# Second attention of a four-layer kernel: the global keys as a block diagonal, the exponentials of the globals as stationary operand

## What is computed

```python
Q = (x @ Wq.T + bq).reshape(Bb, Ll, H, Dh)      # H = 16 heads of Dh = 8, Ll = 256 tokens, 16 batches
K = (x @ Wk.T + bk).reshape(Bb, Ll, H, Dh)
V = (x @ Wv.T + bv).reshape(Bb, Ll, H, Dh)
...
s_loc = jnp.einsum('blhd,blwhd->bhlw', Q, Kw) * scale       # Kw: the 65 keys around each query
a_loc = jax.nn.softmax(s_loc, axis=-1)
local = jnp.einsum('bhlw,blwhd->blhd', a_loc, Vw)
Kg = K[:, global_indices]                                   # 25 global keys
Vg = V[:, global_indices]
s_g = jnp.einsum('blhd,bghd->bhlg', Q, Kg) * scale
a_g = jax.nn.softmax(s_g, axis=-1)
glob = jnp.einsum('bhlg,bghd->blhd', a_g, Vg)
out = 0.7 * local + 0.3 * glob
return out.reshape(Bb, Ll, Dm) @ Wo.T + bo
```

## Time and profile before

| | us |
|---|---|
| median of 3 runs | 1109.99 (1107.80 to 1113.35) |
| the profiled execution | 1111.69 |
| its span in the trace | 1109.9 |
| PE busy | 961.9 (87%) |
| DVE busy | 784.3 (71%) |
| POOL busy | 681.8 (61%) |
| ACT busy | 578.1 (52%) |

### The profile page before, as it was taken

One profiled execution on the slowest core, in us unless ns is written; L12 is line 12 of the kernel. 1 busy time (PEld: TensorE's weight loads), 2 busy tenths in 40 slices (PEclk: granted clock), 3 DMA queues, 4 the chain that ended last, 5 costly groups with the idle time before them and its releaser, 6 DMA issues.

```text
span 1109.9 us, 27990 instructions
## 1 busy us (share of the span) xinstructions
PE 961.9 (87%) x7664; PEld 709.4 (64%) x7664; DVE 784.3 (71%) x3615; ACT 578.1 (52%) x1250; POOL 681.8 (61%) x1491
## 2 busy tenths in 40 slices
PE   2999999999959995899999999999999419999950
PEld 1777777777734552677777777777776317877730
DVE  3788888888826786457776878777776327888845
ACT  2466676666621432255555555555555107777734
POOL 3566666666631222266768787888878623777765
PEclk9899999999978998599999999999999659999985
DMA  6121211111032442121112121222111157777717
GB/s 182 27 52 27 49 40 35 45 30 45 23 133 88 170 152 86 29 49 28 47 29 59 38 59 37 60 55 59 52 40 36 43 177 226 240 252 245 234 56 212
DMA packets 71376, 98.36 MB, mean 89 GB/s; under 512 B 13688, under 2 KB 43256, under 8 KB 71104
## 3 DMA queue, kind: packets, MB, share of 16 engines
q1 hardware_dynamic: 61040, 83.31, 25.6%
q0 software_dynamic: 4992, 10.30, 2.7%
q10 hardware_dynamic: 5232, 3.42, 1.2%
HBM read 49.48 MB, written 24.77 MB: 67 GB/s over the span
## 4 chain that ended last, share of the span: by engine, by line
PE 74%; DVE 9%; issue 6%; SPq 3%; DMA 3%; POOL 2%; ACT 2%; DVEq 0%; ACTq 0%; POOLq 0%
PE bank L348 6%; PE bank L172 5%; PE bank L253 4%; PE bank L357 4%; PE bank L378 4%; PE bank L1499 4%; PE bank L1500 4%; PE bank L1501 4%; PE bank L1265 4%; PE bank L412 4%; PE bank L419 3%; PE bank L168 3%; PE bank L352 3%; PE bank L387 3%; PE bank L404 2%
## 5 line engine op out<-in xcount | busy, mean ns | idle before, releaser
L536 ACT ACTIVATE p<-bank 128x480 f32<-128x480 f32 (+1 forms) x448 | 240.4, 540 | 256.3 <-PE bank L378 101.0
L671 DVE CUSTOM_DVE_ANT_0 bank<-bank,band 128x160 f32<-128x160 f32 x512 | 157.1, 348 | 80.7 <-PE bank L348 67.9
L671 DVE CUSTOM_DVE_ANT_0 bank<-bank,causal 128x128 f32<-128x128 f32 (+1 forms) x512 | 169.8, 388 | 56.4 <-PE bank L352 40.6
L901 POOL TENSOR_SCALAR_AFFINE_SELECT p<-p 128x380 f32<-128x380 f32 (+1 forms) x256 | 146.6, 602 | 63.2 <-ACT p L536 62.3
L1677 POOL DMA_INDIRECT y_rows<-p,rows x92 | 108.3, 1177 | 64.0 <-DVE p L1630 42.7
L671 DVE DVE_READ_ACCUMULATOR2_ANT nm<- 128x1 f32 x1024 | 145.5, 142 | 0.1
L882 POOL TENSOR_SCALAR_AFFINE_SELECT p<-p 128x256 f32<-128x256 f32 (+1 forms) x192 | 91.1, 486 | 69.1 <-ACT p L536 64.2
L348 PE MATMUL bank<-ks,qs 128*128 128x186 f32 x512 | 116.2, 311 | 3.1 <-issue 1.6
L348 PEld LDWEIGHTS bank<-ks,qs 128*128 128x128 f32 x512 | 79.6, 196 | 35.9 <-issue 21.0
L378 PE MATMUL bank<-qs,ks 128*128 128x160 f32 x512 | 100.4, 299 | 0.0
L1570 ACT ACTIVATE p<-bank,wb 128x512 f32<-128x512 f32 x92 | 63.6, 691 | 39.4 <-PE bank L1501 24.3
(11 more groups left out here) (209 smaller groups left out, 2369.0 us busy)
## 6 DMA issues: line engine op xcount, KB each, us to landing
qs<-parts SPq DMA_DIRECT2D x46, 512.0 KB
qs<-qf SPq DMA_DIRECT2D x128, 128.0 KB, 2.4
rows<-xr SPq DMA_DIRECT2D x23, 260.0 KB
parts<-ks SPq DMA_DIRECT2D x8, 512.0 KB
xs<-x_b SPq DMA_DIRECT2D x16, 256.0 KB
p<-in_w SPq DMA_DIRECT2D x12, 256.0 KB
xin<-in_x SPq DMA_DIRECT2D x16, 128.0 KB, 2.2
parts<-qf SPq DMA_DIRECT2D x4, 512.0 KB
```

Source lines behind the costliest of these rows:

```text
L536: act.activation(pb[:, :, :].rearrange("p u c -> p (u c)")[:, lo:lo + cols], bank[:, 0:cols], ACT.Exp, scale=SCALE).then_inc(L.exp_done, 1)
L671: return dve.tensor_tensor_reduce(at, at, mask, -1.0, -BIG, ALU.add, ALU.min, nm[:, item:item + 1])
L901: pool.affine_select(out=at, in_=at, compare_op=ALU.is_ge, fill=0.0, base=base, pattern=[[0, 4], [sign, hi - lo]], channel_multiplier=-sig ...
```

## The change

All of it lies in the second attention.

- The global keys are written by DVE as a block diagonal, `T.kg[p]`, 128 x (4 x 32) for each t, in one masked operation (`lay_out_kg`, behind unit (1,2)), one iteration after `keep_kg`. `keep_kg` now has two operations instead of three, and each signals `kg_kept`: pass one (0,0) waits for the first, (0,2) for the second.
- The scores of the globals are four fp32r matmuls of 256 columns in each batch, two in unit (2,3) and two in unit (3,3), each with 128 outputs. They read the queries as they were before their spreading, `T.qf`, which becomes a ring of three; so the rows of the maxima are sent to `qf` too, by a second DMA in each quarter. Units (0,3) and (1,3) of pass two are gone.
- Their exponentials are two of 512 columns instead of four of 256. The product with the values, `global_values`, has the exponentials stationary and the masked values (64 columns) moving: eight fp32 matmuls at (0,0) of the next iteration, behind `round_pj`. Its result has tokens on the partitions, so the copy `ogs` and `round_og` are gone, and DVE reads PSUM bank 7 in `normalise`.
- `keep_vg` is one operation instead of four, and `keep_array_busy` issues two matmuls instead of four.
- The diagonal keys and two parts of the `qf` ring share memory with buffers of the last layer.

```diff
+    def unit2(self, i, j, u):
+
+        if not self.local:
+            return 3 * (4 * i + j - 3) + u
+        if i == 0:
+            return u
+        return 3 + 14 * (i - 1) + (0, 3, 6, 10)[j] + (u if j < 3 or i < B else u - 3)
...
+    def pass2_unit(self, local, j, u):
+
+        if local and u == 3:
+            return self.late and j > 1
+        return self.pass2[j] and u < 3
...
-        def round_og():
-            bank_read("og", i, p, th)
-            pe.wait_ge(L.ov_kept, L.kept * fin + 2)
+        def global_values():
+
+            pe.wait_ge(L.exp_done, L.unit2(i - 1, 3, 3) + 1)
+            pe.wait_ge(L.vg_kept, fin + 1)
+            wait(pe, L.on_done, fin)
             for tau in range(2):
-                for r in range(2):
-                    m = turn(T.mi[0][:, (2 * tau + r) * P:(2 * tau + r + 1) * P],
-                             T.ogs[:, r, tau * P:(tau + 1) * P])
-            m.then_inc(L.ot_done, 1)
+                out = T.og[:, tau * S:(tau + 1) * S].rearrange("p (r t z) -> p r t z", r=2, t=4)
+                for t in range(4):
+                    m = pe.matmul(out[:, :, t, :], T.pg[t // 2][:, t % 2 * S + tau * P:t % 2 * S + (tau + 1) * P],
+                                  T.vgb[p][:, t, :].rearrange("p (r z) -> p r z", r=2),
+                                  start=tau == 0 and t == 0, stop=True, skip_group_check=True)
+            m.then_inc(L.pg_done, 1)
...
-            for _ in range(4):
+            for _ in range(2):
                 pe.matmul(T.s1[0][:, 0:P], T.ident[:], T.ident[:], start=True, stop=True)
...
-                    pe.wait_ge(L.kg_kept, i + 1)
+                    pe.wait_ge(L.kg_kept, 2 * i + 1)
+            if L.local and u == 2 and j == 0:
+                pe.wait_ge(L.kg_kept, 2 * i + 2)
...
+            unit = L.unit2(i, j, u)
+            bank = T.s2[unit % 2 if L.local else (j + u) % 2]
...
+                pe.wait_ge(L.mrow[js], L.q_base + L.rows_sent * (batch + 1))
...
             if L.local and u == 3:
-                for t in range(4):
-                    m = pe.matmul(bank[32 * t:32 * t + 32, 0:S], T.kg[par][:, t, :], q[:, t, :].bitcast(F32),
-                                  start=True, stop=True)
+                pe.wait_ge(L.kd_done, i)
+                for c in range(2):
+                    t = 2 * (j - 2) + c
+                    m = pe.matmul(bank[:, c * S:(c + 1) * S], T.kg[n][:, t, :], T.qf[(i - 1) % 3][:, t, :],
+                                  start=c == 0, stop=True, skip_group_check=True)
...
-            if part == 2:
-                if j == 0:
-                    pe.wait_ge(L.vg_kept, i)
-                pe.wait_ge(L.exp_done, 4 * step + 4)
-                m = pe.matmul(T.og[:, r * S:(r + 1) * S], T.vgb[n][:, j, :], pb[:, 3, 0:S],
-                              start=j == 0, stop=False, skip_group_check=True)
...
-                if j == 0 and u == 2 and th.finish and L.local:
-                    round_og()
+                if j == 0 and u == 0 and th.finish and L.local:
+                    global_values()
...
+                if th.pass2_unit(L.local, j, u):
                     pass2(j, u)
-                if th.late and u > 0:
+                if th.late and u in (1, 2):
...
-            if L.local:
-                act.copy(T.ogs[:, :, :], T.og[:, :].rearrange("p (r q) -> p r q", r=2)).then_inc(L.ov_kept, 1)
...
-                act.copy(T.qf[:, :, tau * P:(tau + 1) * P], from_).then_inc(L.q_kept, 1)
+                qf = T.qf[(i + 1) % 3 if L.local else 0]
+                act.copy(qf[:, :, tau * P:(tau + 1) * P], from_).then_inc(L.q_kept, 1)
...
+            if L.local and u == 3:
+                wait(act, L.pg_done, i - 1)
+                act.activation(T.pg[j - 2], bank[:, :], ACT.Exp, scale=SCALE).then_inc(L.exp_done, 1)
+                return
...
-            glob = T.mi[0][:, :].rearrange("p (h c) -> p h c", c=16)
+            glob = T.og[:, :].rearrange("p (h c) -> p h c", c=16)
...
-            dve.wait_ge(L.ot_done, L.kept * fin + 2)
+            dve.wait_ge(L.pg_done, fin + 1)
...
-            wait(dve, L.pv_done, 4 * (i - 1))
-            vg = T.mi[1][:, 0:D].rearrange("p (t r s d) -> p r s t d", t=4, r=2, s=2)
-            out = T.vgb[p][:, :, :].rearrange("p (r s) (t z c) -> p r s t z c", r=2, t=4, z=2)
-            mask = T.diag[:, :].rearrange("p (t d) -> p t d", t=4)
-            for s in range(2):
-                for r in range(2):
-                    m = dve.tensor_tensor(out[:, r, s, :, s, 0:DH], vg[:, r, s, :, :], mask, ALU.mult)
-            m.then_inc(L.vg_kept, 1)
+            wait(dve, L.pg_done, i - 1)
+            vg = T.mi[1][:, 0:D].rearrange("p (t j d) -> p t j d", t=4, j=4)
+            out = T.vgb[p][:, :, :].rearrange("p t (j c) -> p t j c", j=4)
+            mask = T.diag[:, :].rearrange("p (o j d) -> p o j d", o=1, j=4).to_broadcast([P, 4, 4, DH])
+            dve.tensor_tensor(out[:, :, :, 0:DH], vg, mask, ALU.mult).then_inc(L.vg_kept, 1)
 
         def keep_kg():
 
 
             dve.wait_ge(L.kg_done, i + 2)
             kg = T.mi[1][:, 0:4 * 32].rearrange("p (t g) -> p t g", t=4)
-            for lo in (0, NGE + S):
-                dve.tensor_copy(T.ks[n][:, :, lo:lo + NGE], kg[:, :, 0:NGE])
-            dve.tensor_scalar(T.kg[n][:, :, 0:NG], kg[:, :, 0:NG], T.rows[:, 0:1], None,
-                              ALU.add).then_inc(L.kg_kept, 1)
+            dve.tensor_scalar(T.ks[n][:, :, 0:NGE], kg[:, :, 0:NGE], T.rows[:, 0:1], None, ALU.add).then_inc(L.kg_kept, 1)
+            dve.tensor_copy(T.ks[n][:, :, NGE + S:KW], kg[:, :, 0:NGE]).then_inc(L.kg_kept, 1)
...
+        def lay_out_kg():
+
+
+            wait(dve, L.p2_done, L.unit2(i - 1, 3, 3) + 1 if i > 1 else 0)
+            own = [P, 4, 4, NG]
+            keys = T.ks[p][:, :, 0:NG].bitcast(F32).rearrange("p t (o g) -> p t o g", o=1).to_broadcast(own)
+            mask = T.diag[:, ::DH].rearrange("p (a j o) -> p a j o", a=1, o=1).to_broadcast(own)
+            dve.tensor_tensor(T.kg[p].rearrange("p t (j g) -> p t j g", j=4)[:, :, :, 0:NG], keys, mask,
+                              ALU.mult).then_inc(L.kd_done, 1)
...
                     normalise()
                 if j == 2 and u == (2 if L.local else 0) and th.finish:
                     residual()
+                if j == 1 and u == 2 and L.local and th.scores:
+                    lay_out_kg()
...
+                if L.local:
+                    qf = T.qf[(i - 1 if j == 0 else i) % 3]
+                    sp.dma_start(qf[32 * js + 24:32 * js + 24 + L.parts, :, :].bitcast(F32),
+                                 T.mt[js][0:4 * L.parts, :].bitcast(F32)).then_inc(L.mrow[js], 16)
...
-    ninth = np.zeros((4, 32, 4, 4, 2, 16), np.float32)
-    for t in range(4):
-        for j in range(4):
-            ninth[t, 0:NG, j, t, j % 2, DH] = 1.0 / W_GLOBAL
+    ninth = np.zeros((4, 32, 4, 4, 16), np.float32)
+    for j in range(4):
+        ninth[j, 0:NG, :, j, DH] = 1.0 / W_GLOBAL
...
+        later = sb("later", [P, XRING * 4 * XW], F32R)
+
+        def part_of(lo, width):
+            return later[:, lo:lo + 4 * width].rearrange("p (t s) -> p t s", t=4)
+
+        T.qf = [qf[:, :, :], part_of(0, S), part_of(4 * S, S)]
+        T.kg = [part_of(8 * S, P), part_of(8 * S + 4 * P, P)]
+        T.pg = [T.p[k][:, 3, :] for k in range(2)]
         T.pick, T.pick4 = sb("pick", [P, 2, NGE], F32R), sb("pick4", [P, 2, 4, 32])
-        T.vgb = [sb(f"vgb{i}", [P, 4, P]) for i in range(2)]
+        T.vgb = [sb(f"vgb{i}", [P, 4, 4 * 16]) for i in range(2)]
```

81 lines of the change are left out of this document (40 added, 41 removed).

## The result

The changed kernel takes 1180.1 us (median of four runs, 1174.5 to 1181.8), the kernel before 1109.6 beside it: ratio 1.062, 95% interval 1.058 to 1.067. The forecast was 1112.7, its range ended at 1121. The profiled execution took 1181.66 us, its span 1179.9.

The account below looks back on a forecast made before the run. PE was busy all but 0.3 us of each iteration, but a VectorE, GpSimd, VectorE chain was as long. Early -7.65, late +7.0, end +3.3: +2.7 on the median 1110.0 gave 1112.7 us, range 1099 to 1121.

Parts of the forecast that it names:

- the clock falls: Rival, slower: PE 86% busy loses its upper clock; one iteration at 1.2 GHz gives about 1130 us; chance 0.06.
- iterations 2, 3: Early iterations without routing: (1,1) starts 1.4 us late, 2.45 us removed behind it; -1.05 us each.
- iterations -1 to 1: First iterations, with no `global_values`: matmuls, filler and copies removed from PE give -0.95, -1.05 and -3.4 us.
- iteration 4: The even iterations' chain of waits, without the DMAs: -0.2 us.
- even late: Even iterations from 5 to 14: 1.8 us delay less 0.8 given back, +1.0 us each.
- odd late: Odd iterations from 5 to 14: (3,1) starts 1.3 us late, 0.95 removed behind it; +0.4 us each.
- The string: Chain VectorE, GpSimd, VectorE from the maxima of (0,2) to the global keys; claimed to start 1.8 us later.
- The 0.15 between `xb` and the residual: Slack ahead of VectorE's residual in even iterations, claimed to absorb about 0.15 us of the 1.8 us delay.
- 1.0 + 3.3 = 4.3: Last iterations: +1.0 us for an even one, +1.8 in iteration 15 and +1.5 in 17, together +3.3.
- Weight loads: Rival, slower: each of 16 `global_values` records costs 0.15 us, 2.4 in all; 1121 us; chance 0.2.
- columns: Rival, faster: moving columns alone price `global_values`, 1.05 us in all; 1102.6 us; chance 0.18.
- PE stays the bound: Rival, faster: the other engines have slack, each iteration from 2 to 14 gains PE's 2.2 us; 1076 us; chance 0.1.

Follow-up runs that it names:

- experiment 6: Changed kernel with filler products at all three places where PE idles: 1123.9 us; with the late even iterations' layer norm also moved behind `keep_kg`: 1119.0 us.
- experiments 1 and 7: Changed kernel with four filler products per iteration end instead of two: 1177.7 us; changed kernel with `global_values` at the previous iteration's end, no filler added: 1141.9 us.
- experiment 7: Changed kernel with `global_values` at the previous iteration's end, filler at PE's waits and late even layer norm one unit earlier: 1148.5 us.

## Why the prediction was wrong

**The step that failed** is the rival "the clock falls": 0.06 of the chances and one iteration at the lower level, 1130 us. It was read from two windows, 6.75 of 10 us busy with a clock of 0.84 and 7.28 with 0.99, as if the busy share of 10 us decided, and the sum itself has no term for the clock. The forecast's own sum gave 86% busy against 99% in the earlier trace rows, and it named waits that come back every iteration. The trace of before spoke both ways: it has waits of that kind at a clock of 1.00 (four of 0.85 to 1.21 us from 358 to 396 us, in another part of the program, and 1.15 at 829), but none above 0.5 us in the iterations from 500 to 825 us, and the filler in the earlier trace rows was a sign that someone had needed it. What the runs showed in its place: taking work off PE is enough to lose the clock, at places that leave no long wait. Without its filler the kernel before itself falls again and again (0.90 to 0.97 in the windows, 1131.4 us), and the changed kernel spent 156 of 400 us at the lower level, which cost at least 56 us. The rival's size was wrong as well: it had one iteration at the lower level, where falls came back in every window from 500 to 900 us.

**The terms, with the clock held** (the kernel of experiment 6 with the layer norm last):

| | forecast | measured |
|---|---|---|
| `global_values` | 1.8 | 1.70 |
| (0,3) on VectorE after pass one (0,0) | 7.68 | 7.73 |
| idle PE ahead of the second projection | 1.4 late | 1.39 |
| iterations 2, 3 | -1.05 (23.2) | -1.1 (23.16) |
| iterations -1 to 1 | -5.4 | -5.9 (see below) |
| iteration 4 | -0.2 | +1.0 (26.59 against 25.60) |
| even late | +1.0 (26.6) | +1.1 (26.70); +1.9 or +2.0 where the layer norm is held |
| odd late | +0.4 (25.8) | +0.6 (25.99) |
| `lay_out_kg` | 0.66 to 1.14, covered | 0.57, covered |

Not all of this is sharp. Iterations -1 to 1 end anywhere from 490.5 to 494.7 us in the profiled runs of variants that are alike up to there, against 498.4 before. In the even late ones pass one starts straight behind the filler, 0.4 us after VectorE's first key operation is done, so up to 0.4 of the 26.70 can be filler.

The string is right: GpSimd's split starts 1.85 us later than in the earlier trace rows, `xb` 1.99. The 0.15 between `xb` and the residual was not given back: the residual starts 17.99 us after pass one against 15.99. Iteration 4 was mis-sized by 1.2; the likely reason, not tested, is that it has the even string and nothing of what the early ones save. At pass one of iteration 14 the two profiled executions stand 0.1 us apart, and 5.3 lie behind it, where the forecast had 1.0 + 3.3 = 4.3. Nearly all of it, 5.1, lies behind pass one of iteration 15, so the end was mis-sized by about 2; in the profiled run with the layer norm in its old place it is 10.8. So with the clock held and that collision out of the way the forecast's 1112.7 became 1119.0 (filler included).

**The other rivals.** Weight loads (0.15 a record) and columns (0.066) are both refuted: it is 0.106 us a record, between the two and where the earlier trace rows put it. "PE stays the bound" is refuted, since PE idles 1.3 to 2.5 us at three places.

**A term that was missing** is the collision of experiment 6. The forecast asked who would be late and not what a string that is late by 1.8 us would then lie beside.

What stays open: the end of the second attention was not looked into. And what sets off a single fall is not shown: gaps of 1.39 us went by without one, one came with nothing longer than 0.27 us ahead of it, and these runs don't separate how the length of the gaps, their number and their place weigh.

## What to carry to other kernels

Where the program holds PE's clock by being dense, work taken off PE is no gain until the engine that binds next is faster too: first lay the saved time out as gaps, place by place, and if the clock then falls, the price can be a multiple of the whole saving (here 70 us, against the 29 that the most hopeful rival gave). Test it by filling each new gap with products nobody reads, at places where another engine is late anyway; what remains after that is the change's own worth, less what the filler costs. When a string of work shifts, look up what each of its operations will lie beside, above all VectorE's operations from and to SBUF against GpSimd's.

## What was not expected of the hardware

- The clock fell with PE busy 96% of the time: the kernel before without filler has 47.92 of 50 us busy and one gap of 0.92 an iteration, and a granted clock of 0.90 in that window; with its filler, at 48.9 to 49.4 of 50 in the windows from 500 to 800 us, it is 1.00. But the busy share alone doesn't tell: windows of 45.5 and 44.0 of 50 us, with gaps of 1.4 us in them, had 1.00 too (experiments 1 and 7). The Trainium skill (TensorE: Matmul & The Clock Gate, A second HAM failure mode: psum-queue depth-cycling) tells of short pauses of PE between groups of matmuls that make the clock swing between its levels; these traces agree, with pauses of mostly 0.6 to 2.6 us ahead of the falls and one of 0.27; many such pauses passed without a fall.
- A fall lengthens PE's work, and waits that stand behind stretched work get shorter (0.15 in place of 1.39 us): the share of busy time (44.6 to 47.3 of 50 us) doesn't show the loss. The number of matmul records in a window does.
- Of two subtract-and-multiply operations of VectorE of 0.34 us each, one took up to 2.24 us beside four gapless masks on GpSimd (experiment 7, layer norm one unit earlier), and ended just behind the last of them. The kernel before has it in two of its iterations, where the two together take 2.77 and 2.17 us.
